# One block more between load and store in two convolutions, and both scan sweeps in one pipeline

## What is computed

```python
# L1: over rows and over columns, and each of them again backwards
dt = jax.nn.softplus(dts + dt_b[None, :, :, None])
a = jnp.exp(dt[..., None] * A[None, :, :, None, :])
b = (dt * u)[..., None] * Bs.transpose(0, 1, 3, 2)[:, :, None]
_, h = jax.lax.associative_scan(comb, (a, b), axis=3)      # h = a * h + b
ys = jnp.einsum('bkdln,bknl->bkdl', h, Cs) + Dsk[None, :, :, None] * u
# L2, first half
t = t + img2tok(_dwconv(tok2img(t), cpe1_w, cpe1_b))        # cpe1
tn = _ln(t, n1_g, n1_b)
act_res = jax.nn.silu(tn @ actproj_w + actproj_b)
ti = tn @ inproj_w + inproj_b
ti = jax.nn.silu(img2tok(_dwconv(tok2img(ti), dwc_w, dwc_b)))   # dwc
```

## Time and profile before

| | us |
|---|---|
| median of 3 runs | 3899.55 |
| lowest and highest run | 3897.82 and 3903.65 |
| the profiled execution | 3894.08 |
| its span, first to last instruction | 3892.3 |

### The profile page before, as it was taken

One profiled execution on the slowest core, in us unless ns is written; L12 is line 12 of the kernel. 1 busy time (PEld: TensorE's weight loads), 2 busy tenths in 40 slices (PEclk: granted clock), 3 DMA queues, 4 the chain that ended last, 5 costly groups with the idle time before them and its releaser, 6 DMA issues. The chain is left out here.

```text
span 3892.3 us, 53786 instructions
## 1 busy us (share of the span) xinstructions
PE 2998.4 (77%) x17500; PEld 1615.2 (41%) x17500; DVE 2489.5 (64%) x2565; ACT 2366.1 (61%) x2681; POOL 1088.2 (28%) x612
## 2 busy tenths in 40 slices
PE   3678766969968876697996877677898778768699
PEld 2344334435534432543553433343454334344355
DVE  5677546876568644787466964578735886466871
ACT  3788434458778743546777864443767876444485
POOL 0235002632034500363103530046210452014530
PEclk9899988989989998898998999888999999988899
DMA  2001454600200146350020024644002004455201
GB/s 67 12 1 33 117 136 147 164 9 0 74 17 0 38 118 191 107 144 9 0 90 1 0 74 110 188 119 107 9 9 81 0 0 112 110 167 143 67 0 49
DMA packets 137194, 274.36 MB, mean 70 GB/s; under 512 B 17139, under 2 KB 93622, under 8 KB 137014
## 3 DMA queue, kind: packets, MB, share of 16 engines
q1 hardware_dynamic: 137014, 272.01, 25.3%
HBM read 194.07 MB, written 77.88 MB: 70 GB/s over the span
## 5 line engine op out<-in xcount | busy, mean ns | idle before, releaser
L1472 DVE SCALAR_TENSOR_TENSOR work<-region,cols,work 128x768 f32<-128x768 f32 x288 | 392.1, 1361 | 15.1 <-DVE work L1472 7.5
L664 POOL TENSOR_TENSOR region<-region 128x768 f32<-128x768 f32 x96 | 211.0, 2201 | 370.8 <-ACT region L844 365.1
L995 PE MATMUL psum<-region,m_fc 128*128 128x384 f32 (+1 forms) x768 | 282.2, 490 | 11.2 <-ACT work L946 11.2
L1241 PE MATMUL psum<-work,m_fc 128*128 128x384 f32 x768 | 282.6, 491 | 0.0
L995 PE MATMUL psum<-region,m_cen 128*128 128x384 f32 (+1 forms) x384 | 165.6, 557 | 136.5 <-DVE region L1585 62.3
L625 POOL TENSOR_TENSOR work<-work 128x768 f32<-128x768 f32 x48 | 113.9, 2377 | 501.8 <-ACT work L764 415.2
L1391 DVE SCALAR_TENSOR_TENSOR work<-region,cols,work 128x768 f32<-128x768 f32 x144 | 202.3, 1430 | 78.3 <-POOL work L625 62.3
L639 POOL TENSOR_TENSOR work<-work,region 128x768 f32<-128x768 f32 x96 | 174.3, 1816 | 235.0 <-DVE work L1406 235.0
L995 PE MATMUL psum<-work,m_avg 128*128 128x384 f32 x576 | 225.5, 516 | 15.6 <-ACT work L806 7.7
L217 DVE SCALAR_TENSOR_TENSOR region<-region,cols 128x768 f32<-128x768 f32 x192 | 223.8, 1166 | 16.7 <-POOL region L664 8.7
L678 POOL COPY region<-work 128x768 f32<-128x768 f32 x4 | 3.3, 823 | 818.6 <-DVE work L1509 818.6
(11 more groups left out here) (234 smaller groups left out, 7495.6 us busy)
## 6 DMA issues: line engine op xcount, KB each, us to landing
work<-scratch_cpe SPq DMA_DIRECT2D x192, 196.0 KB, 3.8
work<-scratch_dwc SPq DMA_DIRECT2D x192, 196.0 KB, 3.8
work<-scratch_lepe SPq DMA_DIRECT2D x192, 196.0 KB, 3.9
region<-in_tab_ch SPq DMA_DIRECT2D x48, 768.0 KB, 5.3
region<-in_x SPq DMA_DIRECT2D x48, 384.0 KB, 3.3
region<-in_tab_tok SPq DMA_DIRECT2D x48, 384.0 KB, 3.1
out<-work SPq DMA_DIRECT2D x48, 384.0 KB, 2.3
scratch_cpe<-region SPq DMA_DIRECT2D x44, 392.0 KB, 4.6
```

What stands on the lines that cost most here:

```text
L664: g.tensor_tensor(chain_tile(conv, n, p), chain_tile(conv, n - 1, p), chain_tile(conv, n, p), ALU.add).then_inc(tap_done[n], 1)
L995: last = pe.matmul(psum[:, bank + s, 0:HC], weights[:, :], moving(s), start=(n == 0), stop=(n == len(terms) - 1))
L1241: last = pe.matmul(psum[:, 4 + s, 0:HC], fc2[:, P * j:P * (j + 1)], static(tile(4 + j))(s), start=(j == 0), stop=(j == 3))
L1472: v.scalar_tensor_tensor(out=by_row(tile(acc + p)), in0=prow(k, b, *TAPS[n]), scalar=tap_weight(conv, TAPS[n]), in1=by_row(tile(acc + p)), ...
```

## The change

In cpe1 and dwc SP's load of block b comes in step b + 3 in place of b + 2, so that it stands behind the store of block b + 2, while it still asks for the stores of b and b + 1 alone. The wait for b itself, which only the first block had, is gone: each store now waits first until the store two blocks back (on the same semaphore) has landed, and so the first blocks' landing is known too. In the scan the two `pipelined` calls of each engine become one call of a new function `chained` over 24 blocks, in which sweep two's first block follows sweep one's last one without a drain. Where a wait for block b - 2 (or b - 1) reaches back over the boundary, `scanned` waits for the first sweep's semaphore at block 12 - 2 + b. PE's wait between the sweeps goes, and so does ACT's second table load. The number of blocks, buffers, matmuls, activations and DMAs is the same.

```diff
+def chained(eng, count, stages):
+    deepest = max(lag for lag, _ in stages)
+    def step(t):
+        for lag, stage in stages:
+            if 0 <= t - lag < 2 * count:
+                stage((t - lag) // count, (t - lag) % count, (t - lag) % 2)
+    for t in range(deepest + 2):
+        step(t)
+    for sweep, (start, stop) in enumerate(((deepest + 2, count), (count + deepest + 2, 2 * count))):
+        pairs = (stop - start) // 2
+        if pairs >= 2:
+            with eng.Fori(0, pairs, 1) as k:
+                for u in range(2):
+                    for lag, stage in stages:
+                        stage(sweep, 2 * k + (start + u - lag - sweep * count), (start + u - lag) % 2)
+            start += 2 * pairs
+        for t in range(start, stop + deepest + (2 if sweep == 0 else 0)):
+            step(t)
...
+        def scanned(eng, i, sweep, key, b, back):
+            if sweep == 1 and isinstance(b, int) and b < back:
+                eng.wait_ge(c_sets[0][key], done(i, NB - back + b))
+            else:
+                eng.wait_ge(c_sets[sweep][key], done(i, b - back))
...
                 def rows_landed(stored, b, p):
-                    if is_first(b):
-                        sp.wait_ge(stored[p], landed(i, b, p))
-                        sp.sem_inc(rows_seen, 1)
                     if not (isinstance(b, int) and b == NB - 1):
                         sp.wait_ge(stored[1 - p], landed(i, b + 1, 1 - p))
                         sp.sem_inc(rows_seen, 1)
 
+                def stored_before(stored, b, p):
+                    if not (isinstance(b, int) and b < 2):
+                        sp.wait_ge(stored[p], landed(i, b - 2, p))
+                        sp.sem_inc(rows_seen, 1)
+
                 def store_x(b, p):
+                    stored_before(x_stored, b, p)
                     sp.wait_ge(d_out, done(i, b))
...
                 def store_ti(b, p):
+                    stored_before(ti_stored, b, p)
...
-                pipelined(sp, NB, [(2, load_x_shifted), (0, store_x)])
-                pipelined(sp, NB, [(2, load_ti_shifted), (0, store_ti)])
+                pipelined(sp, NB, [(3, load_x_shifted), (0, store_x)])
+                pipelined(sp, NB, [(3, load_ti_shifted), (0, store_ti)])
...
-                    if sweep == 0:
-                        pipelined(g, NB, [(0, du)])
-                    else:
-                        pipelined(g, NB, [(2, add_y), (0, du)])
+                chained(g, NB, [(2, add_y), (0, du)])
...
-                    a.preload_act_table_set("natural_log_exp_and_others")
-                    pipelined(a, NB, [(2, decay), (0, soft)])
+                a.preload_act_table_set("natural_log_exp_and_others")
+                chained(a, NB, [(2, decay), (0, soft)])
...
-                    all_done(pe, i, b_act if sweep == 0 else c_sets[0]["step"])
-                    pipelined(pe, NB, [(3, bc), (0, dt)])
+                all_done(pe, i, b_act)
+                chained(pe, NB, [(3, bc), (0, dt)])
...
-                    pipelined(v, NB, [(3, input_term), (3, scan), (3, outputs), (1, step_size)])
+                chained(v, NB, [(3, input_term), (3, scan), (3, outputs), (1, step_size)])
```

More of the change, by code:

```diff
@@ L769, in middle, with soft @@
                 pipelined(a, NB, [(0, first_terms), (3, silu_u)])
-                for sweep in range(2):
+                def soft(sweep, b, p):
                     c = c_sets[sweep]
[L774 to L792, removed]
-                    a.preload_act_table_set("natural_log_exp_and_others")
-                    pipelined(a, NB, [(2, decay), (0, soft)])
@@ new lines, in soft, with decay @@
+                    a.wait_ge(c["exp"], done(i, b))
+                    a.activation(tile(p), tile(p), ACT.Ln, bias=col("one")).then_inc(c["log"], 1)
+                def decay(sweep, b, p):
+                    c = c_sets[sweep]
+                    a.wait_ge(c["step"], done(i, b))
+                    if sweep == 0 or is_first(b) or (isinstance(b, int) and b == 1):
+                        scanned(a, i, sweep, "hc", b, 2)
+                    else:
+                        a.wait_ge(c["y"], done(i, b - 2))
+                    a.activation(tile(4 + p), tile(p), ACT.Exp, scale=col(f"l1_A{sweep}")).then_inc(c["decay"], 1)
@@ L1396, in middle, with step_size, input_term @@
                 pipelined(v, NB, [(2, scan_tap_stage(n)) for n in (2, 3, 4)])
-                for sweep in range(2):
+                def step_size(sweep, b, p):
+                    c = c_sets[sweep]
+                    v.wait_ge(c["log"], done(i, b))
+                    v.wait_ge(c["relu"], done(i, b))
+                    v.tensor_tensor(halves(tile(p)), halves(tile(p)), pair(2 * p), ALU.add).then_inc(c["step"], 1)
+                def input_term(sweep, b, p):
+                    c = c_sets[sweep]
+                    v.wait_ge(c["du"], done(i, b))
+                    v.wait_ge(c["B"], done(i, b))
+                    v.tensor_tensor(bu_flat, tile(2 + p), bu_flat, ALU.mult).then_inc(c["bu"], 1)
@@ L1399, in middle, with scan @@
+                def scan(sweep, b, p):
                     c = c_sets[sweep]
                     edge = BLK - 1 if sweep == 0 else 0
[L1402 to L1418, removed]
-                        v.tensor_tensor_scan(way(tile(6 + p)), way(tile(4 + p)), way(bu_flat), initial=start,
-                                             op0=ALU.mult, op1=ALU.add).then_inc(c["h"], 1)
@@ L1422, in outputs @@
[L1422 to L1429 removed]
+                    v.wait_ge(c["bu"], done(i, b))
+                    v.wait_ge(c["decay"], done(i, b))
@@ new lines, in scan, with outputs @@
+                    start = col("zero") if is_first(b) else tile(7 - p)[:, edge:edge + 1]
+                    way = (lambda ap: ap) if sweep == 0 else (lambda ap: ap[:, ::-1])
+                    v.tensor_tensor_scan(way(tile(6 + p)), way(tile(4 + p)), way(bu_flat), initial=start,
+                                         op0=ALU.mult, op1=ALU.add).then_inc(c["h"], 1)
+                def outputs(sweep, b, p):
+                    c = c_sets[sweep]
+                    v.wait_ge(c["h"], done(i, b))
+                    v.wait_ge(c["C"], done(i, b))
+                    y = flat(3, b) if sweep == 0 else tile(4 + p)
+                    v.tensor_tensor(halves(y), halves(tile(6 + p)), pair(6), ALU.mult).then_inc(c["hc"], 1)
```

58 lines of the change are left out of this document (28 added, 30 removed).

## The result

| | before | after |
|---|---|---|
| median of the runs, us | 3898.69 (4 runs) | 3771.05 (4 runs) |
| lowest and highest run | 3892.62 and 3903.65 | 3766.47 and 3777.05 |
| profiled execution | 3894.08 | 3766.47 |
| its span | 3892.3 | 3764.7 |
| mean granted TensorE clock | 0.92 | 0.926 |

The changed kernel takes 0.9674 of the time of before, 95% interval 0.9659 to 0.9689: 127.6 us less. The forecast was 147.6 us less. The spans differ by 127.6 us too, so the two profiled executions can stand for the runs.

A forecast was written before the change was run, and what follows sets the result against it. The prediction took the landing of a store issued one instruction earlier to be in every block's loop in cpe1 and dwc. Savings of 27 + 41.6 + 79 = 147.6 us from the median of 3899.55 gave 3752 us, range 3735 to 3796.

The forecast's parts named there:

- the signs of being wrong: TensorE still waiting for scratch transfers in cpe1, loads over 8 us, or stages after dwc lengthening by what dwc gave.
- Rival 3: cpe1 and dwc: the queue's own throughput paces, blocks stay at 7.1 us, only the scan gains; 3873 us, chance 4%.
- Scan, 27 forecast: Scan: removing the drain and refill between the sweeps leaves 56 us an image, saving 27 us; bounds 24 and 30.
- their 5.1: Scan: four table loads of 1.28 us, 5.1 us if not hidden by ScalarE's wait for TensorE; counted as nothing.
- cpe1, 41.6 forecast: cpe1: steps fall from 7.1 to 5.9 us, saving 10.4 us an image, 41.6 in all; bounds 30 and 46.
- the forecast's 11.1 and 2.7 less: cpe1: the last two steps stay at 11.1 us, or about 2.7 us shorter where the clock holds.
- the normalisation's loop: cpe1: the centring product of block b waits for the normalisation of b - 2, holding steps at 5.9 us.
- dwc, 79 forecast: dwc: the same edit saves 19.7 us an image, 79 us in all; bounds 60 and 92.
- 6.15 forecast for each: dwc's drain: two buffers bind, so a conv starts 6.15 us after the end of the conv two blocks back.
- Rival 2: The queue binds: a load takes 8.7 us for 6.15, dwc loses about 11 us an image; 3796 us, chance 12%.
- Rival 1: dwc's drain: half clock, convs of 4.10 us, 12 us less gained; 3763 us, chance 25%.
- Rival 4: cpe1 and dwc: the clock falls to half over both stages, making the kernel slower; 3963 us, chance 3%.

The follow-up runs named there:

- in cpe1 alone: Kernel of before with only cpe1's later load and gated stores: 3855.27 us, ratio 0.9904.
- in dwc alone: Kernel of before with only dwc's later load and gated stores: 3831.53 us, ratio 0.9834.
- the reordered kernel: Changed kernel with cpe1's averaging product one block earlier and after the conv, and ScalarE's root first in a step: 3737.07 us, ratio 0.957.
- the two runs with its old code: Kernel of before with only the scan's sweeps joined, 3870.37 us, and with only cpe1's later load and gated stores, 3855.27 us.
- Half the bytes: Changed kernel with the shifted loads of cpe1 and dwc cut to half their width: 3731.59 us, ratio 0.9561.

## Why the forecast came out so

The forecast was 3752 us and the kernel takes 3771.05, within the range of 3735 to 3796. The mechanism was as told in all three parts. The size of dwc's drain was off, and 14.5 us in unchanged code had no term.

**What bounded it.** That the landing of a store paced each block of both stages held: without it (in cpe1 alone, in dwc alone) the waits fell and the time with them. Of the signs of being wrong, TensorE's waits for transfers in cpe1 fell from 50.2 to 4.5 us, no load of dwc's drain took over 7.6 us to its conv, and the stretches after dwc grew by 6.2 us where dwc gave 72.2. Rival 3, that the queue's throughput paced it at 7.1 us a block, is out by the same runs.

**Scan, 27 forecast, 28.2 measured.** Each pair of first scans stands 55.7 us apart; that is nearer to all steps at 4.61 (55.3, the bound) than to the 56 taken. Four of the eight table loads are gone, which the forecast counted as nothing; the 1.2 us over leaves little room for their 5.1, though they were not tried alone. The mechanism named, drain and refill, isn't all of it: before, the stretch between the first scans had the full clock in image three alone (granted 1.00, 61.2 us), and 0.95, 0.97 and 0.95 in the others (63.6, 62.7, 63.6); after, all four have 1.00. So 251.1 - 4 x 61.2 = 6.3 of the 28.2 us go with the clock, by this reckoning, and 22 with the drain and refill.

**cpe1, 41.6 forecast, 41.7 measured, closer than the terms were.** The first six steps of image three are 5.90 to 6.15 us, mean 6.04, and the next three 5.77: nine come to 53.6, where the forecast had 53.1. The last two took 7.16 + 2.61 = 9.8 us there, the middle of the forecast's 11.1 and 2.7 less; in image four, with the clock granted in full, they took 8.4. And the mean of before over four images is 73.45, not the 73.25 of the two that the forecast used. These differences of 0.2 to 0.5 us an image cancel, which is luck. That the next bound would be the normalisation's loop, and not TensorE, is the step that mattered, and the reordered kernel shows it: steps of 5.0 to 5.1 without a byte or an instruction less.

**dwc, 79 forecast, 72.2 measured.** The working can be followed in image three. Conv 0 starts at 2350.91 and conv 5 ends at 2377.45, 26.5 later (26.6 forecast). Then conv 7 starts 6.6 after conv 5's end, conv 9 starts 6.15 after conv 7's, conv 11 starts 6.4 after conv 9's (6.15 forecast for each), and the lengths are 3.59, 3.10 and 2.17, mean 2.95, between the 2.17 and 4.10 of the earlier trace rows: sums over 52.4 us, against the middle of 52.1. The other images took 53.2, 55.2 and 53.0. In image two, the longest, the convs of the drain are these (x96 is two convs without idle time between them), after a conv 5 that ends at 1452.37:
```profile
1459.97 5.82 PE L1047 MATMUL psum<-work,m_dwc_shifted 64*32 64x384 f32 x96 [4.07 <-DMA work<-scratch_dwc]
1469.62 5.80 PE L1047 MATMUL psum<-work,m_dwc_shifted 64*32 64x384 f32 x96 [3.82 <-DMA work<-scratch_dwc]
1479.62 3.71 PE L1047 MATMUL psum<-work,m_dwc_shifted 64*32 64x384 f32 x48 [4.20 <-DMA work<-scratch_dwc]
```
In the mean of the four images it is 53.45, 1.35 longer than forecast; and the kernel of before, of which the forecast used images one and three (71.85), has a mean of 71.5 over all four. (1.35 + 0.35) x 4 = 6.8 us. The term that was mis-sized is the wait in the drain: from the end of one conv to the start of the conv two blocks on, which the forecast took as 6.15 us, it is 5.9 to 7.7 over the four images, mean 6.66. That is three times 0.5, or 1.5 us an image; the convs' lengths, 2.9 in the mean for 3.13, give part of it back. The drains stand at a DMA share of 0.88 to 0.97, while the rows that gave 6.12 were of a stretch in which transfers filled 61.6%. The 72.2 itself hangs on one trace of before: against the 278.8 us that dwc took in the two runs with its old code, it would be 65.

Rival 2, a queue that binds, came in small part, and in the drain alone: it had a load at 8.7 us, and the wait is 6.66 for 6.15, with each load still issued only when its buffer is free. Half the bytes gave 35 us there, and nothing in cpe1 or in the first six convs, which stand 4.88 us apart in both. Rival 1, half clock throughout the drain, is half true: convs of 2.17 stand beside some of 3.1 to 3.6 in image three. By the rule of the Trainium skill ("TensorE: Matmul & The Clock Gate", "HAM oscillation") that the prediction weighed, all would have been 4.10; the trace doesn't agree, with a mean of 2.95. Rival 4, a clock that falls in both stages, did not come: 1.00 in the first part of dwc, and 0.97 to 1.00 in cpe1.

**What had no term: 14.5 us in unchanged code.** It is the difference between 142.1 and 127.6. The stretches from sweep two's first scan to cpe1's first normalisation are 5.0 us longer over four images, those from cpe1's last to dwc's first sum 3.2, and from dwc's end to the next image's scan, or the end, the differences are -3.7, +1.9, +4.3 and +3.7. Where the work in a window is the same, the clock shows. From cpe1's last normalisation to dwc's first sum in image three, before and after (as in the windows above):
```profile
2399.00:2431.80 32.80, 23.80 (x105) 11.90 (x106) 10.09 (x10) 9.42 (x10) 0.00 (x0) 0.95 0.36 98
```
```profile
2318.80:2353.20 34.40, 25.37 (x105) 12.62 (x106) 10.12 (x10) 9.42 (x10) 0.00 (x0) 0.90 0.38 106
```
The same 105 matmuls take TensorE 1.57 us longer at a granted clock of 0.90 than at 0.95, and the stretch is 1.6 us longer. Before, two images had 0.95 here and two 0.90; after, all four have 0.90, and that is the 3.2 us. The first conv of cpe1 likewise went from 2.17 us to 3.3 or 3.4 in three images, and from 3.11 to 2.17 in the fourth. So the clock's low stretches moved, with both signs. No run held the clock fixed, so what moved them, and whether all 14.5 us are theirs, stays open. The 4.6 us between the profiled execution and the median are spread of the runs.

In sum 3771.05 - 3752 = 19 us: 6.8 of dwc, -1.2 of the scan, -0.1 of cpe1, 14.5 of the rest, and -0.9 since the forecast stood on a median of 3899.55 and the comparison's is 3898.69.

## What to carry to other kernels

When a load asks for a store that was issued just ahead of it on the same queue, the store's landing is in the loop; place the load one store later and give the store the wait instead. Before sizing the gain, look for a place in the same trace where that wait is already absent: the interval there is near the next bound. Here it was 5.8 to 5.9 us, the steps came to 6.0, and TensorE's own work would have allowed 5.0. In dwc, where the products stop before the convolutions do, the end goes at the pace of its transfers, and a smaller lag shortened it without any other cost. And a stage's length read from one trace can be off: here by 7 us of 286 for unchanged code.

## What the runs showed of the hardware

- A landing time depends on what else the queue carries. The same 392 KB store lands 4.6 us after its issue where the loads around it are 4 x 196 KB, and 2.5 us where they are half that; the loads themselves take 4.1 and 2.3.
- TensorE's busy share doesn't tell its clock. In the drain, busy 17.39 of 30 us (58%), it was granted 0.89; in the drain of before, busy 24.17 of 43 us (56%), 0.65. The busy time is itself longer at a lower clock: the first window has 328 matmuls, the second 295.
- The order of steps in a loop body cost 9.6 us in cpe1 of image three (63.3 against 53.7), with TensorE's matmuls unchanged.
